# Two transformer layers on one core: exps and maxima taken two PSUM banks at a time, and a slot's extra pieces moved in front of its PV products

## The reference

```python
xn = _layernorm(x)
x = x + attn0(xn) + moe(xn)      # RoPE, 16 heads of 8, no mask; 8 experts, top 2, 128 -> 512 -> 128
xn = _layernorm(x)
x = x + attn1(xn) + ffn(xn)      # causal, 16 heads of 8; FP4-rounded gate/up/down, 128 -> 352 -> 128
# attention, per head:
scores  = einsum('bhqd,bhkd->bhqk', Q, K) / sqrt(8)
weights = softmax(scores)
out     = einsum('bhqk,bhkd->bhqd', weights, V)
```

## Time and profile before

| | |
|---|---|
| median of three runs | 1646.52 us (1646.3 to 1650.8) |
| the profiled execution, its own time | 1650.6 us |
| its span | 1648.9 us |
| granted TensorE clock, mean | 0.944 |
| TensorE busy (matmuls) | 1477.5 us, 90% |
| VectorE busy | 1342.0 us, 81% |
| ScalarE busy | 1131.9 us, 69% |
| GpSimd busy | 579.7 us, 35% |
| DMA | 131.80 MB, 80 GB/s |

### The profile page before, as it was taken

One profiled execution on the slowest core, in us unless ns is written; L12 is line 12 of the kernel. 1 busy time (PEld: TensorE's weight loads), 2 busy tenths in 40 slices (PEclk: granted clock), 3 DMA queues, 4 the chain that ended last, 5 costly groups with the idle time before them and its releaser, 6 DMA issues.

```text
span 1648.9 us, 34553 instructions
## 1 busy us (share of the span) xinstructions
PE 1477.5 (90%) x10685; PEld 623.0 (38%) x10685; DVE 1342.0 (81%) x3450; ACT 1131.9 (69%) x2612; POOL 579.7 (35%) x532
## 2 busy tenths in 40 slices
PE   3688989997999999998999999989999989889996
PEld 1121334442434554433343444334444433334432
DVE  7999877786887778898888878879887878887990
ACT  2167678786788556777878756767887845766675
POOL 4003302003063353733434361221624473644520
PEclk8599999998999989999999999999999987999998
DMA  8202264323263135231711225223462100500000
GB/s 246 56 7 60 78 164 116 89 80 89 55 180 96 35 113 127 69 89 49 185 39 44 63 61 152 66 82 103 147 137 65 39 24 1 154 2 15 2 2 14
DMA packets 162915, 131.80 MB, mean 80 GB/s; under 512 B 30825, under 2 KB 130098, under 8 KB 162738
## 3 DMA queue, kind: packets, MB, share of 16 engines
q1 hardware_dynamic: 158642, 121.19, 27.2%
q0 software_dynamic: 4096, 8.40, 1.7%
HBM read 88.50 MB, written 40.50 MB: 78 GB/s over the span
## 4 chain that ended last, share of the span: by engine, by line
PE 64%; DVE 18%; ACT 6%; issue 5%; POOL 4%; DMA 1%; SPq 1%; another core or an unknown queue 0%; DVEq 0%; ACTq 0%; POOLq 0%
PE ring L504 41%; PE pO L504 19%; DVE mparts L1149 10%; PE ring L507 4%; ACT PR L808 4%; DVE junk L1153 1%; ACT hid L875 1%; DVE xn L1216 1%; DVE xr L1329 1%; DVE hs L1441 1%; DVE stats L1199 1%; DVE hs L1440 1%; POOL rstd L700 1%; POOL ra L707 0%; POOL parts L715 0%
## 5 line engine op out<-in xcount | busy, mean ns | idle before, releaser
L808 ACT ACTIVATE PR<-ring 128x512 f32<-128x512 f32 (+3 forms) x1792 | 875.9, 557 | 279.8 <-PE ring L504 267.1
L1149 DVE TENSOR_REDUCE mparts<-ring 128x1 f32<-128x512 f32 x1280 | 806.8, 682 | 122.1 <-PE ring L504 108.6
L504 PE MATMUL pO<-PR,VX 128*18 128x512 f32 (+3 forms) x3584 | 444.7, 569 | 9.2 <-ACT PR L808 8.5
L504 PE MATMUL ring<-KX,QX 48*128 48x512 bf16 (+3 forms) x1792 | 339.4, 373 | 82.3 <-ACT PR L808 32.4
L504 PE MATMUL ring<-QX,KX 50*128 50x512 bf16 (+3 forms) x1792 | 335.7, 371 | 36.7 <-DVE mparts L1149 20.3
L504 PEld LDWEIGHTS ring<-QX,KX 50*128 50x128 bf16 x1792 | 89.6, 93 | 481.7 <-DVE mparts L1149 175.2
L1153 DVE CUSTOM_DVE_ANT_0 junk<-ring,diag 128x384 bf16<-128x384 f32 (+3 forms) x512 | 227.8, 486 | 53.6 <-PE ring L504 46.3
L504 PEld LDWEIGHTS ring<-KX,QX 48*128 48x128 bf16 x1792 | 96.5, 94 | 181.5 <-DVE mparts L1149 54.1
L758 POOL TENSOR_SCALAR bq<-bq 128x352 f32<-128x352 f32 (+1 forms) x40 | 47.1, 1177 | 333.9 <-ACT bq L912 322.7
L731 POOL DMA_INDIRECT rows_in<-xn,at x64 | 62.6, 978 | 257.2 <-PE pO L504 166.0
L875 ACT ACTIVATE hid<-ring,b1r 128x128 f32<-128x128 f32 x368 | 104.9, 369 | 36.8 <-PE ring L504 36.2
(11 more groups left out here) (164 smaller groups left out, 1406.1 us busy)
## 6 DMA issues: line engine op xcount, KB each, us to landing
scratch<-parts SPq DMA_DIRECT2D x96, 256.0 KB, 3.7
w1r<-in_w SPq DMA_DIRECT2D x92, 256.0 KB
w2r<-in_w SPq DMA_DIRECT2D x92, 256.0 KB
QX<-scratch SPq DMA_DIRECT2D x128, 96.0 KB, 3.2
KX<-scratch SPq DMA_DIRECT2D x64, 192.0 KB, 4.0
xg<-rows_in SPq DMA_DIRECT2D x92, 64.0 KB
rows_out<-yx SPq DMA_DIRECT2D x92, 64.0 KB
QX<-mT SPq DMA_DIRECT2D x256, 2.0 KB
```

The lines of the kernel that those rows point to most:

```text
L504: return nc.tensor.matmul(dst, lhsT, rhs, start=start, stop=stop, **kw)
L808: nc.scalar.activation(PR[:, n % 2, HALF * j + off:HALF * j + HALF], ring[plan.bank("E", k)][:, off:HALF], ACT.Exp, scale=SCALE).then_inc( ...
L1149: v.tensor_reduce(dst, src[:, 0:w], axis=X, op=ALU.max).then_inc(s_mr, 1)
```

## The change

Three things change.

1. The exps of a pair (two banks) become one instruction of 128 x 2 x 512, and so do the maxima of a pair where no mask is applied. Both wait for both matmuls of the pair, and both banks of the pair are given back when the one instruction ends. The masked maxima (line 1153 before) stay single.
2. The two banks of a pair must lie side by side. The ring gives way to a table: `place_banks` goes through the pairs and extras in the order of TensorE and picks for each the bank or the neighbouring two banks that were used longest ago, looking five places ahead (`choose`). `vacant` now waits for whatever the chosen bank held before (`plan.was`).
3. In each slot the extras move from the end to the place between M0 and PV, on TensorE, ScalarE and VectorE. On ScalarE the exps of S1 come behind the extras, on VectorE the maxima of M1, the combine and the later small steps do.

```diff
-            for pair in range(2):
-                for kind, key, n in (("E", s["step"], self.steps), ("M", s["quad"], self.quads)):
...
+            self.pairs(s, 0)
             for e in s["xs"]:
...
-                self.at["X"][k] = len(self.ring)
                 self.ring.append(("X", e))
...
+            self.pairs(s, 1)
...
+    def choose(self, used, units, now):
+        if not units:
+            return 0, None
+        width = units[0]
+        places = sorted(range(RING - width + 1), key=lambda b: max(used[b:b + width]))[:4]
+        best = None
+        for b in places:
+            ago = now - max(used[b:b + width])
+            then = used[:b] + [now] * width + used[b + width:]
+            cost = max(0, 4 - ago) ** 2 + self.choose(then, units[1:], now + 1)[0]
+            if best is None or cost < best[0]:
+                best = cost, b
+        return best
+
+    def place_banks(self):
+        units = [self.ring[i:i + (1 if self.ring[i][0] == "X" else 2)] for i in range(len(self.ring))
+                 if self.ring[i][0] == "X" or self.ring[i][1] % 2 == 0]
+        used, holds = list(range(-RING, 0)), {}
+        self.banks, self.was = {}, {}
+        for now, unit in enumerate(units):
+            b = self.choose(used, [len(u) for u in units[now:now + 5]], now)[1]
+            for i, item in enumerate(unit):
+                self.banks[item] = b + i
+                self.was[item] = holds.get(b + i)
+                holds[b + i] = item
+                used[b + i] = now
...
+        def both(kind, k, lo, hi):
+            a, b = plan.bank(kind, k), plan.bank(kind, k + 1)
+            return ring_all[:, :].rearrange("p (b n) -> p b n", n=HALF)[:, a:b + 1, lo:hi]
...
-                    for j in js:
-                        k = 4 * n + j
-                        act.wait_ge(s_e, k + 1)
-                        nc.scalar.activation(PR[:, n % 2, HALF * j + off:HALF * j + HALF],
-                                             ring[plan.bank("E", k)][:, off:HALF], ACT.Exp,
-                                             scale=SCALE).then_inc(s_ex, 1)
+                    k = 4 * n + js[0]
+                    act.wait_ge(s_e, k + 2)
+                    dst = PR[:, n % 2, HALF * js[0]:HALF * js[0] + 2 * HALF].rearrange("p (j n) -> p j n", n=HALF)
+                    nc.scalar.activation(dst[:, :, off:HALF], both("E", k, off, HALF), ACT.Exp,
+                                         scale=SCALE).then_inc(s_ex, 2)
...
-                    r = plan.at[kind][k] - RING
-                    if r >= 0:
-                        was, of = plan.ring[r]
+                    if plan.was[kind, k]:
+                        was, of = plan.was[kind, k]
...
+                    if layer == 0 or P * (qt + 1) > HALF * (kh + 1):
+                        k, i = 4 * plan.quads[s["quad"]] + js[0], TH * (js[0] // 2) + qt % TH
+                        dve.wait_ge(s_m, k + 2)
+                        v.tensor_reduce(mparts[layer][:, qt // TH, i:i + 2 * TH + 1:2 * TH, kh], both("M", k, 0, HALF),
+                                        axis=X, op=ALU.max).then_inc(s_mr, 2)
+                        return
```

More of the change, by code:

```diff
@@ L295, in number, with pairs @@
                     self.pools[e[1:-1]] = len(self.pools)
-    def bank(self, kind, k):
-        return self.at[kind][k] % RING
+        self.place_banks()
+    def pairs(self, s, pair):
+        for kind, key, n in (("E", s["step"], self.steps), ("M", s["quad"], self.quads)):
+            if key is not None:
+                for j in (2 * pair, 2 * pair + 1):
+                    k = 4 * n[key] + j
+                    self.ring.append((kind, k))
+    def bank(self, kind, k):
+        return self.banks[kind, k]
+    def choose(self, used, units, now):
[23 more added lines that the diff above has]
+                used[b + i] = now
 PLAN = Plan()
@@ L972, in _ @@
                     maxima(s, 0)
[L973 to L994, removed]
                     for e in s["xs"]:
-                        vacant("X", plan.xs[e])
+                        vacant("X", e)
                         dst = bank(e)
@@ L1115, in _ @@
                         ins.then_inc(s_x, 1)
+                    if s["pv"] is not None:
+                        p, g, qh, kt = s["pv"]
+                        n = plan.steps[s["pv"]]
+                        last_kt = plan.kts(p, qh) - 1
+                        off = 0 if PHASES[p][0] == 0 else max(0, P * (kt - TH * qh))
+                        if g == 0 and qh == 0 and kt == 0:
+                            for h in range(NH):
+                                pe.wait_ge(*freed(("v", p, h)))
+                        if n == 0:
+                            pe.wait_ge(s_zero, 1)
+                        pe.wait_ge(s_ex, 4 * (n + 1))
+                        first = kt == 0 and g % 2 == 0
+                        if first and plan.outs[p, g // 2, qh]:
+                            pe.wait_ge(s_oT, plan.outs[p, g // 2, qh])
+                        for j in range(G):
+                            h = G * g + j
+                            ins = mm(pO[OW * j:OW * j + 2 * VC, off:HALF], values(p, h, kt),
+                                     PR[:, n % 2, HALF * j + off:HALF * j + HALF],
+                                     start=first, stop=kt == last_kt and g % 2 == 1, skip_group_check=True)
+                        ins.then_inc(s_pv, 1)
+                    scores(s, 1)
+                    maxima(s, 1)
             @block.vector
@@ L1380, in _ @@
                         small_step(e)
[L1381 to L1389, removed]
                     for e in s["xs"]:
@@ L1454, in _ @@
                             v.tensor_tensor(sums(n), sums(n), left(n), ALU.add).then_inc(s_sum, 1)
+                    maxima(s, (2, 3))
+                    if s["combine"] is not None:
+                        layer = PHASES[s["combine"][0]][0]
+                        dve.wait_ge(s_mr, 4 * (plan.quads[s["quad"]] + 1))
+                        v.tensor_reduce(mneg[:, :], mparts[layer][:, s["combine"][2], :, :], axis=X, op=ALU.max,
+                                        negate=True).then_inc(s_ng, 1)
+                        dve.wait_ge(s_ng, plan.combines[s["combine"]] + 1)
+                    for e in s["small"][2]:
+                        small_step(e)
                     for e in s["small"][3]:
```

27 lines of the change are left out of this document (10 added, 17 removed).

## The result

The changed kernel takes 1948.55 us (median of 4 runs, 1938.96 to 1955.42) against 1646.41 for the kernel before: the ratio is 1.183, with a 95% interval of 1.177 to 1.189. It is slower by 302 us. The forecast was 1857 us, 211 more than today, in a range from 1740 to 1950. So the median lies at the very edge of the range, and two of the four runs lie beyond it.

The account below looks back on a forecast made before the run. TensorE, busy for 90% of the span, was taken as the bound. Steps 938 + 305, extras 426, lead and end 87 gave 1756; additions made 1866, less 5 is 1861 profiled, so 1857 us; range 1740 to 1950.

Parts of the forecast that it names:

- The mechanism: In each full slot, with extras moved ahead of PV, M0 waits 0.86 us for S1's merged exp; chance 0.72.
- R1: Rival: today's waits are VectorE's, order does not matter, merged maxima save time; 1614 us, at the far bound 1550; chance 0.05.
- R2: Rival: new wait falls where TensorE waits anyway; within 2% of 1646 us, up to 1680; chance 0.03.
- The round trip: From S1's start until its banks are free for M0: 0.49 + 1.04 + about 0.10 = 1.63 us.
- the masked steps: Shorter steps, 32 of each width: waits before M0 of 0.40, about 0.25, 0.07 and 0 us.
- The 435 cases: Count from the plans: in 435 of 448 cases M0's pair takes its banks from the previous slot's S1.
- term a: TensorE reaches `mtr` at 1.94 us after S1, but `mneg` is ready some 2.25 after; 64 x 0.3 = 20 us.
- The base: The same sum for today's kernel, with 2.07 us per full slot and no masked waits: 1456 us against 1649.
- The rest on top: Added to 1756 us: clock 50, late expert rows and weights 20, copy of `pO` ahead of S1's exps 20.
- The clock: Today at half for 8% of the steps' 1562 us window, about 50 us lost; the forecast carried this 50 over.
- R3: Rival: idle gaps in each slot drop the clock, half for 27% of the time; 135 us more, 1990; chance 0.12.
- R4: Rival: VectorE runs 0.5 us late for 170 extras taking a bank of M1; 85 us more, 1940; chance 0.08.

## Why the prediction was right, and where it was off

**The mechanism was right.** M0 waits for the exp of the S1 three pairs back, since the move takes the extra out of the gap between them. It follows from the distance, which sits at 1.71 us in the changed kernel, 1.22 with single banks and 1.28 with half an exp, and from the extra's return, which takes away most of the loss. *R1* (VectorE's waits are what counts) is wrong: its own sign, a median distance under 1.0 us, is not there, and with 37 us less work on VectorE the old order was no faster. *R2* (little change) is wrong by the 18%.

**The round trip** was put at 1.63 us and is 1.71: a merged exp, which waits for both matmuls, starts 0.54 us after S1, where single ones start 0.48 after it, and its release takes 0.145 instead of 0.10. The exp itself (1.023) was right to 0.02. That the earlier trace rows seemed to show nearly the same, 1.61 us from S1 to M0, was chance. There the ring makes M0 wait for one exp only, which takes 1.22 us (the move alone shows it), and the rest is a copy of `pO` that ScalarE made first:

```profile
1052.82 0.60 ACT L510 ACTIVATE oT<-pO 128x512 f32<-128x512 f32 x1
```

The waits in front of M0 come to 362 us where 298 were forecast. The 0.08 us account for some 25 of the 64; the masked steps took about 50 us where 23 were forecast; the remaining ten or so are not explained.

**The 435 cases** in which M0 takes its banks from S1 were counted too coarsely: 317 take both and 118 take only one. It made no difference to the forecast, since the merged exp holds that bank to the end as well, but it is why single exps gave 45 us back.

**`mtr`** (term a) was mis-sized: 33 us against 20. The wait itself is there as forecast.

**The base** of the sum was 36 us too high: 1456 us for today without waits, where the fastest quarter of each piece gives 1420. This hid a part of the other errors.

**The rest on top,** put at 90 us (clock 50, late data 20, the copy of `pO` 20), is 138; no run separates its parts. Together the terms missed by 64 + 13 + 48 = 125 us, and the base took 36 of them back. That the result still fell inside the range, by 1.5 us, is therefore partly luck.

**The clock.** The granted clock fell: mean 0.944 before and 0.921 after, so at half for 11% and 16% of the span, 185 and 308 us; the forecast kept the share. This is a weak form of *R3*: in the window of the steps the clock went from 0.96 to 0.93, where R3 was priced at 0.86. What it costs can be estimated from the four runs of the changed kernel: 1955 us at 0.919 and 1939 at 0.932, some 1.3 us for 0.001, so that the fall of 0.023 goes with about 30 of the 302 us. With the waits at full clock above, this rules the clock out as the main cause (T3), though the time of 1949 lies nearer to R3's 1990 than to the 1857 of the forecast. The Trainium skill (TensorE: Matmul & The Clock Gate, "A second HAM failure mode: psum-queue depth-cycling") says that short idles between groups that cycle through banks let the clock swing; the traces agree in direction, since the clock is 0.921 with the longest waits, 0.935 with the move alone and 0.949 with the pairs alone (the kernel before has 0.943 to 0.957 over its runs), but no run here separates cause and effect.

*R4*, VectorE late for the extras' banks, was priced at 1940, which is closer to the result than the forecast; only the trace tells them apart, and it has no sign of R4. In front of `unit` and `y` the reductions ended 0.3 us of idle time in all. TensorE's waits in the changed trace (engine and line, releaser, us in total, times, longest):

```profile
PE ring L537 <- ACT PR L846: 270.0, 353, 2.0
...
PE ring L537 <- DVE mparts L1181: 21.4, 38, 1.5
```

The exps ended 270 us of idle time, the reductions 21. (The 270 us in front of the maxima's matmuls, in the section on the result, are another sum that happens to be as large.)

## What to carry over

Work on the bottleneck engine that stands between writing a buffer and needing it again is not overhead but the cover of the buffer's round trip; before moving it, add up what is left between the two, and compare that with the latency of the reader. Merging two short instructions lengthens the time for which both buffers are held, and asking for neighbouring buffers makes the ring shallower: here this cost 3% before anything was merged, and work saved on engines that were not waited for gave nothing back. When a wait is removed, look for the next one in line (here `mtr`). Spreading the fillers more evenly over the slots gained up to 1% here; why is open.

## What the runs showed of the hardware that was not expected

An exp over two banks (128 x 1024, 1023 ns) is hardly shorter than two single ones in a row (1.08 us), and a maximum over two banks (1224 ns) hardly shorter than two (1.29 us). A single exp takes 604 ns, but the second of two in a row adds only 0.48 us, so most of what merging could save is saved already. And although the two matmuls of a pair start 3 ns apart (median), an exp that waits for both starts 0.06 us later than one that waits for the first (0.54 against 0.48 us after S1); why is not shown.
